# A selective scan and two layers of local attention on one Trainium2 core: a new order of the steps for all engines, and a new table of PSUM banks

## The reference, cut to what matters

```python
x = L0_attn_x                                          # (16, 512, 256)
h = layernorm(x) * (1 + ca) + sa
# mixer
x_ssm, z = split(h @ W_in.T)                           # 512 features each
dt = softplus(x_ssm @ W_dt.T + b_dt)
h_t = exp(dt_t * A) * h_{t-1} + dt_t * B_t * x_t       # 512 features x 16 states, 512 tokens
y = (sum over states of h_t * C_t + x_ssm * D) * silu(z)
x = x + ga * (y @ W_out.T)
h = layernorm(x) * (1 + cb) + sb
# stack, DEPTH = 2 layers of
q, k, v = split(shift(x) @ wqkv);  q, k = rotary(l2norm(q) * qs), rotary(l2norm(k) * ks)
x = x + softmax(q k^T over a window of 128 and the one before) v @ wo
a, g = split(layernorm_affine(shift(x)) @ w1 + b1);  x = x + (a * gelu(g)) @ w2 + b2
# result: x1 + gb * stack(h)
```

## Time and profile before

| | us |
|---|---|
| median of 3 runs (4377.27 to 4380.29) | 4378.54 |
| the profiled execution | 4379.32 |
| its span, first to last instruction | 4377.4 |
| PE busy | 4063.1 (93%) |
| DVE busy | 3579.9 (82%) |
| POOL busy | 2617.2 (60%) |
| ACT busy | 2605.6 (60%) |

### The profile page before, as it was taken

How to read it: one execution, slowest core, us unless ns; L and a number is a source line. 1 busy time by engine, 2 the same in 40 slices (tenths; PEclk the granted TensorE clock), 3 DMA queues, 4 the chain that set the end, 5 groups by cost and what they waited for, 6 DMA issues and landing times.

```text
span 4377.4 us, 60024 instructions
## 1 busy us (share of the span) xinstructions
PE 4063.1 (93%) x19614; PEld 2631.7 (60%) x19614; DVE 3579.9 (82%) x5981; ACT 2605.6 (60%) x5703; POOL 2617.2 (60%) x1297
## 2 busy tenths in 40 slices
...
GB/s 95 111 121 116 121 116 122 119 123 116 117 120 120 123 124 111 114 86 15 30 15 30 16 15 30 16 30 49 70 29 20 39 20 34 26 25 35 20 32 23
DMA packets 118498, 295.02 MB, mean 67 GB/s; under 512 B 21208, under 2 KB 43664, under 8 KB 118192
## 3 DMA queue, kind: packets, MB, share of 16 engines
...
...
## 4 chain that ended last, share of the span: by engine, by line
PE 49%; DVE 6%; issue 2%; ACT 1%; POOL 0%; SPq 0%; ACTq 0%; DMA 0%; DVEq 0%; POOLq 0%
PE b_bank L1425 11%; PE b_bank L1314 11%; PE b_bank L1446 6%; PE b_bank L1304 5%; PE b_bank L1391 5%; PE b_bank L1364 4%; PE b_bank L1375 3%; PE b_bank L1344 3%; DVE b_qk_rate L1685 2%; DVE b_qk L1696 1%; ACT b_qk_rot L1475 1%; DVE b_xc L1806 1%; PE b_bank L1405 1%; PE b_bank L1410 1%; DVE b_scores L1744 1%
## 5 line engine op out<-in xcount | busy, mean ns | idle before, releaser
L813 POOL TENSOR_TENSOR a_state<-a_state,a_c_wide 128x1024 f32<-128x1024 f32 x512 | 1196.3, 2367 | 36.6 <-DVE a_state L755 36.6
L573 PE MATMUL a_y_sum<-a_state,a_ident 128*128 128x512 f32 x2048 | 944.5, 599 | 0.7 <-POOL a_state L813 0.6
L1646 POOL TENSOR_TENSOR b_scores<-b_scores,b_row_rate 128x1024 f32<-128x1024 f32 (+1 forms) x256 | 426.6, 1683 | 722.4 <-DVE b_row_rate L1761 722.4
L755 DVE TENSOR_TENSOR_SCAN a_state<-a_decay,a_slot 128x1024 f32<-128x1024 f32 x352 | 788.8, 2271 | 1.8 <-ACT a_decay L684 0.6
L1619 POOL TENSOR_TENSOR b_by_cos<-b_qk,b_rotary 128x1024 f32<-128x1024 f32 x128 | 308.9, 2413 | 593.7 <-DVE b_qk L1696 593.6
L1314 PE MATMUL b_bank<-b_w_qkv,b_hx_part 128*128 128x512 f32 x2304 | 626.2, 412 | 37.5 <-DVE b_w_qkv L1837 18.0
L573 PEld LDWEIGHTS a_y_sum<-a_state,a_ident 128*128 128x128 f32 x2048 | 388.5, 192 | 402.9 <-issue 343.3
L1520 ACT ACTIVATE b_scores<-b_scores,b_row_bias 128x256 f32<-128x256 f32 (+1 forms) x1024 | 478.2, 471 | 200.7 <-DVE b_row_bias L1750 199.2
L684 ACT ACTIVATE a_decay<-a_dt,a_neg_a 128x512 f32<-128x512 f32 x704 | 458.8, 711 | 163.6 <-DVE a_state L755 163.4
L1425 PE MATMUL b_bank<-b_hn_part,b_w 128*128 128x512 f32 x2112 | 508.4, 398 | 7.0 <-DVE b_hn_part L1668 7.0
L1314 PEld LDWEIGHTS b_bank<-b_w_qkv,b_hx_part 128*128 128x128 f32 x2304 | 419.8, 192 | 156.7 <-issue 44.6
...
## 6 DMA issues: line engine op xcount, KB each, us to landing
a_c_wide<-bc_rows SPq DMA_DIRECT2D x256, 512.0 KB, 3.7
...
```

The source lines that it names most:

```text
L573: last = nc.tensor.matmul(y_sum[dd][:], ident[:], state[state_ring.slot[q]][:, i, :], start=False, stop=(j == GROUPS - 1 and i == GROUP - 1))
L755: nc.vector.tensor_tensor_scan(flat(h), flat(factor), flat(term), 0.0, ALU.mult, ALU.add).then_inc(scan_done.sem, 1)
L813: nc.gpsimd.tensor_tensor(h[:], h[:], c_wide[c_ring.slot[q // 2]][:], ALU.mult).then_inc(cmul_done.sem, 1)
L1646: nc.gpsimd.tensor_tensor(probs, probs, row_rate[:, w, at].unsqueeze(2).to_broadcast([P, 4, hi - lo]), ALU.mult)\
```

## The change

It writes both lists of steps in another order and fills the table of banks anew. No step is added or taken away and no function of the kernel is touched. Some steps cross the boundary between two passes (`score:0.0`, `score:0.1`, `score:1.0` and `pn:0.0` now stand at the end of a pass, one sequence ahead, and `ptr:3` in the pass of its own stage).

```diff
 MIXER_ORDER = """
-sum-:5 bcast-:10 sum-:6 mul-:12 mul-:13 xload:0 bcast-:11 scan-:12 cload-:13 cload-:14 cload-:15 scan-:13 cload:0
...
+scan-:11 sum-:5 cmul-:9 mul-:13 bcmid-:0 cload-:15 xload:0 sum-:6 xscopy-:3 cload:0 cload:1 hT-:1 scan-:12 bload:6
...
 ORDER = """
-psq:0 mask:0.1 hxs:0 add:0 ptr-:3 wo:0 prate:0 score:0.0 add:1 rate:0 score:0.1 mask:1.0 pn:0.0 pn:0.1 pss:0 wo:1 vc:0
...
+psq:0 score:1.1 mask:0.0 mask:0.1 wo:0 add:0 hxs:0 wo:1 mask:1.0 pq:0 rate:0 mask:1.1 pn:0.1 add:1 pk:0 pt:0.0 pss:0
...
+gated:0 gelu:1 hh:0 ga:0 hh:1 pn:2.1 gated:1 gelu:2 pt:2.0 ga:1 pt:2.1 exp:3 prot:2 ga:2 gated:2 hh:2 gelu:3 rate:3
...
 BANK_OF = """
...
-pt3_2:5 v3:4 pt3_3:2 y0:2 y1:6
...
+pt2_3:3 g0:3 a0:2 g1:7 a1:3 g2:2 a2:1 g3:7 a3:4 g4:6 a4:0 wd0:6 wd1:4 g5:7 q_t2:2 k_t2:4 q3:3 pt3_0:1 pt3_1:1 pt3_2:7
...
```

More of the change, by code:

```diff
@@ new lines @@
+decay-:17 decay-:18 bcast-:9 cmul-:10 cload:2 bcast-:10 bcast-:11 decay-:19 scan-:13 decay-:20 sum-:7 cmul-:11
+cmul-:12 bcast-:12 mul-:14 xs-:0 mul-:15 sum-:8 soft-:0 cmul-:13 cmul-:14 decay-:21 xs-:1 decay-:22 decay-:23 cload:3
+scan-:14 zcopy-:0 scan-:15 bcrest-:0 cmul-:15 xs-:2 decay-:24 decay-:25 bcast-:13 zcopy-:1 mul-:16 cload:4 mul-:17
+mul-:18 mul-:19 cmul-:16 decay-:26 cmul-:17 sum-:9 bcast-:14 bc-:0 bcast-:15 cmul-:18 scan-:16 decay-:27 scan-:17
+gate-:0 bclow-:0 sum-:10 xs-:3 gate-:1 scan-:18 decay-:28 zcopy-:2 sum-:11 scan-:19 cmul-:19 mul-:20 bcast-:16 mul-:21
@@ L160 @@
+mul:6 cen2:0 mul:7 cmul:3 sum:1 up:1 decay:10 decay:11 cload:13 bcast:6 scan:6 dtadd-:1 xscopy:0 scan:7 decay:12
+decay:13 cmul:4 cmul:5 xscopy:1 mean2:0 scan:8 xT:0 cload:14 decay:14 xn2:0 bload+:1 bcast:7 h2:0 sum:2 mul:8 xscopy:2
+cmul:6 bcast:8 bccopy:0 hcut:0 scan:9 mul:9 sum:3 cmul:7 cmul:8 xT:1 hT:0 mul:10 var2:0 hcut:1 mul:11 sum:4 decay:15
+bcup:0 decay:16 mul:12 scan:10 bload+:4
 """
```

54 lines of the change are left out of this document (22 added, 32 removed).

## The result

The changed kernel takes 4517.1 us (median of 4 runs, 4513.5 to 4520.2), beside 4379.05 us for the kernel before (4377.3 to 4380.3): 3.15% slower, ratio 1.0315 with a 95% interval of 1.0302 to 1.0328. The forecast was 4450 with a range of 4408 to 4520. So direction and range held, and the size was short: +71 us forecast, +138 measured.

A forecast was written before the change was run, and what follows sets the result against it. Mixer passes were taken as bound by DVE, with POOL nearly full, and layer 1 passes by PE. Terms: 4379.3 - 25 (mixer) - 6 (edge) + 103 (second phase) = 4451, median 0.8 lower, so 4450 us; range 4408 to 4520.

The forecast's parts named there:

- Mixer: First phase: DVE's 1.88 us gate wait goes, less 0.3 for other waits, 1.6 us in 16 passes, -25 us.
- Edge of the layers: First pass of layer 2: resload ahead of store on SP's queue removes the wait at wo, -6 us.
- Old waits of the second phase, 2.47 a pass: PE's three waits in a layer 1 pass, 1.3, 0.8 and 0.3 us, all go as banks change.
- `pt:2.1` for `gelu:1`: PE waits 2.25 us for bank 7, which gelu:1 empties behind four table loads on ACT.
- `ptr:2` for the copy behind `exp:3`: PE waits 1.7 us for bank 2, whose copy of pt:2.2 stands on ACT behind exp:3.
- `pt:3.2` for `gated:5`: PE waits 0.35 us for bank 7, freed by gated:5 after three more loads around prate:3.
- `wd:4`, `wd:5`: End of the down projection: PE waits 1.6 us at wd:5 for hl:5, with DVE's rotary product blocked by POOL.
- Without any wait the pass would be 73.82 us: Layer 1 pass, second phase: with the old waits gone only PE's busy time of 73.82 us is left.
- I take both together as zero: Second phase: gain from six half-height runs instead of seven and cost of restarts behind waits together count 0 us.
- rival (c): More waits than found, from DVE's tight copies or POOL's delay by padd:0: 1.5 us a pass more, 4495 us; 20%.
- Rival (d): The mixer gains nothing because POOL's 102.82 us is the bound behind DVE's: 4475 us; 13%.
- Rival (b): Table switches cost 1.38 us of emptying beyond each load, 12 us a pass on top of 3.6: 4830 us; 2%.

The follow-up runs named there:

- e10_gelu5_first: Changed kernel with gelu:5 and gated:5 moved ahead of prate:3 and pnorm:3, three table loads a pass fewer: 4510.8 us, ratio 1.0300.
- e5_two_banks: Changed kernel with two bank entries moved, pt2_1 from 7 to 6 and q_t2 from 2 to 1, same order and loads: 4473.8 us, ratio 1.0216.
- e11_mended: Changed kernel with one load of the Ln and Exp set ahead of rate 2, several steps reordered, pt2_1 and k_t2 in other banks: 4430.3 us, ratio 1.0117.
- e6_one_set: Changed kernel with one explicit load of the set holding Ln and Exp ahead of the Ln of w = 2 and 3: 4414.4 us, ratio 1.0080.
- e12_mended_twice: e11_mended with pt:2.3 and ptc:2 ahead of gated:3, prot:3 ahead of hl:5, and wd0, g5, pt3_2 in other banks: 4336.5 us, ratio 0.9900.
- e7_after_no_gelu: Changed kernel with Identity and the same bias in place of gelu, all table loads of the pass gone: 4278.4 us, ratio 0.9770.

## Why the prediction fell short, point by point

| Step of the prediction | Forecast | Measured |
|---|---|---|
| Mixer | -25 us | -26.4 (run with the mixer alone) |
| Edge of the layers | -6 | -8.1 (run with the edge alone) |
| Old waits of the second phase, 2.47 a pass | go | gone |
| `pt:2.1` for `gelu:1` | 2.25 | 2.3 |
| `ptr:2` for the copy behind `exp:3` | 1.7 | 1.9 |
| `pt:3.2` for `gated:5` | 0.35 | 0.4 |
| `wd:4`, `wd:5` | 1.6 | 1.0 and 0.14 |
| `ptr:0` | 0.2 | 0.3 |
| All waits of this pass | 6.1 | 82.10 - 75.94 = 6.16 |
| PE's work in this pass | 73.82 | 75.94 |
| PE's restarts and clock, second phase | 0 | +61.8 |
| PE's waits, second phase, with the edge | +97 (103 - 6) | +98.0 |

The last two rows are from the first `mean` to the last, before and after (span, then PE's busy time):

```profile
1964.18:4330.87 2366.69, 2278.91 (x14098) 1725.96 (x14099) 1781.68 (x4629) 1341.93 (x3517) 895.82 (x521) 1.00 0.08 28
1943.41:4469.95 2526.54, 2340.72 (x14088) 1742.14 (x14087) 1838.03 (x4629) 1655.65 (x3761) 1020.45 (x521) 0.98 0.08 26
```

**The sum of waits was right**, place by place and in all (87.8 us before, 185.8 after), for the reason given: the loads stand in the chain between two gelu, and a bank ties PE to its end. The runs without gelu and with loads in idle time show both halves of it: with no loads the change is 101 us faster, and with eight more loads in the right place the old order loses nothing. That the total of the waits comes within 1 us is in part chance: in 12 passes an early fall of the clock takes up to 1.2 us off the second wait, and the forecast knew nothing of it.

**The step that failed** is the sentence "Without any wait the pass would be 73.82 us" with the one on restarts, "I take both together as zero". PE's own work was held fixed while waits of 6.1 us were put into it. The runs show two terms there, both in PE's busy time and not in its waits. One is the granted clock, which falls once a pass to 1.2 GHz: 1.54 us for the 14 matmuls behind the second wait (two passes of one kernel, with and without). The prediction does not speak of the clock at all. The other is the restart behind each wait, 0.24 us: six waits in place of three, 0.7 us. The gain from fewer runs of half-height products is at most small: the base without gelu has 73.49 in place of 73.82, and one wait less explains 0.24 of these 0.33. Together 75.94 - 73.82 = 2.1 us in this pass, and 61.8 us from the first `mean` to the last.

That is most of the 67 us that the forecast lacks. Some 6 more lie ahead of the first `mean`, which comes 20.8 us earlier where the mixer alone gives 26.4. What the passes that fill the second phase lose there was not followed.

**Where the range held by luck.** Its upper end was set with +153 for further waits from tight places of DVE, rival (c). There are none: the waits are those forecast. The time of 4517 came close under 4520 for another reason, the clock and the restarts. The lower end is not the sum of its own ends either: the terms have -42 and -6 for mixer and edge and +55 for the second phase, which gives about 4385 and not 4408. With no gain from mixer and edge and the +153, the upper one would be 4532. The forecast pass of 79.5 to 80 us was missed, with 82.10.

**Smaller misses.** The wait at the end of the down projection was placed on `wd:5` for DVE's block and sits on `wd:4` for POOL's: DVE's rotary pair began 0.13 us ahead of `hl:4`, and `hl:4` took 2.27 us on POOL, where in the kernel before such a product takes 1.28 to 1.32. It is the same meeting of the two engines, lost by the other one. The edge gained 2 us more than its wait, since a fall of the clock went with it. The mixer pass is 104.16, a little under the 104.4 to 105 forecast. Rival (d), that POOL's 102.82 us bound the mixer, is refuted: the pass is 104.16 with POOL at 102.74, and the gate's wait of 1.88 is 0.3. Rival (b) fell with the chain of 7.15 us and again with the eight added loads.

**What stays open.** Which waits bring the clock down. By full passes (28 in each kernel), with the waits of a pass of layer 1:

| Kernel | Waits of a pass, us | Longest | Passes with a fall |
|---|---|---|---|
| changed | 6.2 | 2.3 | 28 |
| `e10_gelu5_first` | 6.0 | 2.3 | 28 |
| `e5_two_banks` | 4.4 to 5.1 | 1.6 | 12 |
| `e11_mended` | 4.2 | 2.7 | 15 |
| `e6_one_set` | 3.8 | 1.9 | 8 |
| before | 2.5 | 1.3 | 0 |
| `e12_mended_twice` | 1.9 | 0.8 | 0 |
| `e7_after_no_gelu` | 0.6 | 0.3 | 0 |

Neither the sum nor the longest wait orders them, and in three of these kernels passes with the same waits differ. That the fall belongs to the new order itself is refuted by the runs without gelu and mended twice, which have that order and no fall. No run held the waits fixed and changed their spacing alone.
